# Attention: short score tiles on alternating bank pairs, new hand-written engine orders, and y copied and cleared by GpSimd

## The reference

```python
xn = layernorm(x) * gamma + beta
q, k, v = split(xn @ Wq, xn @ Wkv)            # 16 heads of 64
q, k = rope(q), rope(k)
sim = (q * 64 ** -0.5) @ k.T                  # causal mask
out = (softmax(sim) @ v) @ Wo
```

## Time and profile before

| | |
|---|---|
| device time, median of 3 runs | 2793.81 us (2791.97 to 2796.38) |
| the profiled execution's own time | 2805.46 us |
| its span, first to last instruction | 2803.7 us |
| attention, first A0 to last W3 on TensorE | 945 to 2316 us of the span |
| TensorE busy over the span | 90% |
| mean granted TensorE clock | 0.947 |

### The profile page before, as it was taken

The page is one execution under the profiler, slowest core; times in us unless marked ns, Lnnn a source line. Parts: engine busy times, 40 slices in busy tenths (PEclk is TensorE's granted clock), DMA queues, the critical chain, the costliest instruction groups (busy, mean ns, idle before and its releaser), DMA issues. The chain is left out here.

```text
span 2803.7 us, 45798 instructions
## 1 busy us (share of the span) xinstructions
PE 2537.3 (90%) x14626; PEld 1727.8 (62%) x14627; DVE 1312.9 (47%) x3173; ACT 1146.4 (41%) x2597; POOL 536.0 (19%) x479
## 2 busy tenths in 40 slices
PE   6999997999955699999999999999999995999992
PEld 6454544555535466665666656666666665999992
DVE  5445351122215455555556555655555652333335
ACT  3212111111113366665666656666566661222221
POOL 3000003444423233421111101101101100111113
PEclk7999998999975799999999999999999997999996
DMA  5010104865424422322111121111111106666795
GB/s 192 15 45 30 45 15 158 263 187 162 118 53 135 134 79 82 100 79 68 37 37 37 52 52 37 37 37 52 51 40 37 32 16 249 237 237 240 240 342 198
DMA packets 146334, 298.79 MB, mean 107 GB/s; under 512 B 16720, under 2 KB 104800, under 8 KB 135648
## 3 DMA queue, kind: packets, MB, share of 16 engines
q1 hardware_dynamic: 125280, 254.96, 28.6%
q0 software_dynamic: 20992, 43.07, 5.9%
HBM read 196.13 MB, written 68.30 MB: 94 GB/s over the span
## 5 line engine op out<-in xcount | busy, mean ns | idle before, releaser
L1347 DVE CUSTOM_DVE_ANT_0 at_p<-at_ps,atk_mask 128x640 f32<-128x640 f32 (+7 forms) x512 | 372.5, 750 | 304.3 <-PE at_ps L1201 168.8
L1258 ACT ACTIVATE at_p<-at_p,at_nmax 128x640 f32<-128x640 f32 (+7 forms) x512 | 394.2, 772 | 227.6 <-DVE at_nmax L1347 165.3
L1265 ACT ACTIVATE at_pT<-at_ps 128x512 f32<-128x512 f32 (+1 forms) x640 | 333.8, 550 | 186.1 <-PE at_ps L1211 183.0
L1290 POOL TENSOR_TENSOR at_qkT<-at_raw,at_swapped 128x1024 f32<-128x1024 f32 x64 | 151.3, 2364 | 1086.4 <-DVE at_swapped L1362 1086.1
L1201 PE MATMUL at_ps<-at_qkT 64*128 64x512 f32 (+3 forms) x1536 | 320.3, 522 | 19.3 <-DVE at_nmax L1347 15.3
L1211 PE MATMUL at_ps<-atk_ident,at_p 128*128 128x128 f32 x2304 | 323.6, 277 | 2.6 <-ACT at_raw L1271 1.9
L1211 PEld LDWEIGHTS at_ps<-atk_ident,at_p 128*128 128x128 f32 x2304 | 258.6, 141 | 109.0 <-issue 79.1
L1222 PE MATMUL at_ps<-at_pT,at_v 128*64 128x256 f32 (+1 forms) x2560 | 279.1, 365 | 0.1
L1498 PEld LDWEIGHTS moe_ps<-moe_xT,moe_w 128*128 128x128 f32 x2304 | 270.8, 193 | 5.2 <-ACT moe_xT L1531 1.6
L1498 PE MATMUL moe_ps<-moe_xT,moe_w 128*128 128x128 f32 x2304 | 271.4, 276 | 0.9 <-ACT moe_xT L1531 0.9
L1183 PE MATMUL at_ps<-atk_h,atk_w 128*128 128x512 f32 x512 | 250.3, 622 | 15.5 <-SPq L1074 15.2
(11 more groups left out here) (203 smaller groups left out, 3254.6 us busy)
## 6 DMA issues: line engine op xcount, KB each, us to landing
moe_w<-in_w_w SPq DMA_DIRECT2D x72, 1028.0 KB, 4.4
at_swapped<-at_raw SPq DMA_DIRECT2D x256, 128.0 KB, 2.3
atk_w<-in_w_qkv SPq DMA_DIRECT2D x32, 384.0 KB
slot_in<-ex_zero SPq DMA_DIRECT2D x9, 1032.0 KB
moe_xs<-slot_in SPq DMA_DIRECT2D x72, 129.0 KB
xn_n<-n_stage SPq DMA_DIRECT2D x8, 1024.0 KB, 4.6
ex_wg<-in_w_eg SPq DMA_DIRECT2D x16, 512.0 KB
ex_wu<-in_w_eu SPq DMA_DIRECT2D x16, 512.0 KB
```

The lines of the kernel that those rows point to most:

```text
L1258: act.activation(buf, buf, ACT.Exp, bias=nmax[:, unit:unit + 1], scale=-1.0, accum_out=rsum[:, unit:unit + 1]).then_inc(exp_done, 1)
L1265: act.activation(dst, ring[RING_BANK[part][ev]][:, 0:(i1 - i0) * P].rearrange("p (k c) -> p k c", c=P), ACT.Copy).then_inc(t_read, 1)
L1290: pool.tensor_tensor(out=qkT[x][:, :].rearrange("p (m t) -> p m t", m=2)[:, :, half * CH:(half + 1) * CH], in0=raw[half][:, :].rearrange(" ...
L1347: dve.tensor_tensor_reduce(out=p[unit % LAG][:, 0:(n[0] + 1) * P], in0=scores(*n), in1=mask[:, T - (n[0] + 1) * P:T], scale=-1.0, scalar=3 ...
```

## The change

Three things are changed.

Score tiles 0 to 3 alternate between the two banks of their head: even ones lie in banks 0 and 2, odd ones in banks 1 and 3. Tiles 4 to 7 need both. The wait of S2 and S3 is for the M two tiles back instead of one; S0 and S1 wait for the last M of the pair before. All three orders are new: TensorE's old one changes the array's form 22 times per iteration, the new one 17 times. The third thing is that `end(b)` moves from VectorE to GpSimd. It runs there after both rotations for the first pair of the next sequence, and VectorE's W0.0 waits for the clearing in every iteration, by a sequence number that `act_on` now gets.

```diff
--- before.py
+++ after.py
@@ -956,12 +956,12 @@
 QW = 2 * P
 HD = DH // 2
 
-PE_ORDER = ("T0.0 S2 A0+ T1.0 S3 V0 A1+ T2.0 A2+ T2.1 S4 T3.0 W0 T3.1 S5 A3+ T4.0 T4.1 T4.2 V1 S6 W1 A4+ A5+ T5.0 T5.1 S7 T5.2 T6.0 T6.1 A6+ T6.2 V2 "
-            "T6.3 T7.0 T7.1 T7.2 A7+ T7.3 S0+ W2 V3 S1+ W3")
-ACT_ORDER = ("E2.0 T0.0 T1.0 A0+ E2.1 E3.0 E3.1 A1+ T2.0 V0 T2.1 T3.0 E4.0 E4.1 T3.1 T4.0 E5.0 T4.1 V1 E5.1 T4.2 E6.0 A4+ A5+ E6.1 T5.0 T5.1 T5.2 "
-             "T6.0 T6.1 E7.0 E7.1 T6.2 T6.3 T7.0 T7.1 T7.2 V2 T7.3 E0.0+ V3 E0.1+ E1.0+ E1.1+")
-DVE_ORDER = ("M2.0 I0 M2.1 M3.0 M3.1 A2+ M4.0 M4.1 W0.0 W0.1 A3+ M5.0 M5.1 P0+ I1 I2 M6.0 W1.0 M6.1 W1.1 M7.0 M7.1 A6+ P1+ A7+ P2+ P3+ I3 M0.0+ W2.0 "
-             "M0.1+ W2.1 M1.0+ M1.1+ W3.0 W3.1")
+PE_ORDER = ("S2 S3 T0.0 A0+ T1.0 A1+ T2.0 A2+ T2.1 S4 V0 A3+ W0 S5 T3.0 T3.1 A4+ T4.0 T4.1 V1 S6 T4.2 A5+ W1 S7 T5.0 T5.1 T5.2 T6.0 A6+ T6.1 T6.2 "
+            "T6.3 V2 T7.0 T7.1 T7.2 T7.3 S0+ S1+ W2 V3 A7+ W3")
+ACT_ORDER = ("T0.0 E2.0 E2.1 T1.0 A0+ A1+ T2.0 T2.1 V0 E3.0 E3.1 E4.0 E4.1 T3.0 T3.1 T4.0 A4+ T4.1 E5.0 E5.1 V1 T4.2 E6.0 A5+ E6.1 T5.0 T5.1 T5.2 "
+             "T6.0 E7.0 T6.1 E7.1 T6.2 T6.3 V2 T7.0 T7.1 T7.2 T7.3 V3 E0.0+ E0.1+ E1.0+ E1.1+")
+DVE_ORDER = ("M2.0 M2.1 M3.0 M3.1 M4.0 A2+ M4.1 A3+ I0 W0.0 W0.1 M5.0 I1 P0+ M5.1 P1+ I2 M6.0 M6.1 W1.0 W1.1 M7.0 A6+ M7.1 W2.0 M0.0+ M0.1+ P2+ M1.0+ "
+             "W2.1 M1.1+ I3 P3+ A7+ W3.0 W3.1")
 
 
 def events(order):
@@ -1020,7 +1020,8 @@
 
         def scores(t, e):
 
-            return s.all_banks[:, e * 2 * CH:e * 2 * CH + (t + 1) * P]
+            at = e * 2 * CH + (t % 2 * CH if t < TB // 2 else 0)
+            return s.all_banks[:, at:at + (t + 1) * P]
 
         if scatter:
             rows = [s.sb(f"rows{u}", TB * ROW) for u in range(2)]
@@ -1042,23 +1043,21 @@
 
             return turned_before(n[0]) + n[1]
 
-        def run(eng, act_on, first_done=lambda: None, end=lambda b: None):
-
-            act_on("first", -1, -1, 1)
+        def run(eng, act_on, first_done=lambda: None):
+
+            act_on("first", -1, -1, 1, -1)
             first_done()
             if nb > 1:
                 with eng.Fori(0, nb - 1) as b:
                     with eng.Fori(0, PAIRS // 2) as i:
                         for u in range(2):
-                            act_on("both", b * PAIRS + (i * 2 + u), i * 2 + u, u)
-                    end(b)
+                            act_on("both", b * PAIRS + (i * 2 + u), i * 2 + u, u, b)
             it = (nb - 1) * PAIRS
             with eng.Fori(0, PAIRS // 2 - 1) as i:
                 for u in range(2):
-                    act_on("both", i * 2 + (it + u), i * 2 + u, u)
-            act_on("both", it + PAIRS - 2, PAIRS - 2, 0)
-            act_on("last", it + PAIRS - 1, PAIRS - 1, 1)
-            end(nb - 1)
+                    act_on("both", i * 2 + (it + u), i * 2 + u, u, nb - 1)
+            act_on("both", it + PAIRS - 2, PAIRS - 2, 0, nb - 1)
+            act_on("last", it + PAIRS - 1, PAIRS - 1, 1, nb - 1)
 
         s.start()
         with nc.Block() as block:
@@ -1192,13 +1191,13 @@
                         elif kind == "S":
                             if n % 4 == 0:
                                 pe.wait_ge(rot_done, of * 2 + n // 4 + 1 + ONE)
-                            if part != "first" or n > 0:
-                                pe.wait_ge(max_done, of * UNITS + 2 * n + ONE)
+                            if part != "first" or n > 1:
+                                pe.wait_ge(max_done, of * UNITS + 2 * (n if n >= TB // 2 else max(n - 1, 0)) + ONE)
                             width = (n + 1) * P
                             for at in range(0, width, CH):
                                 to = min(at + CH, width)
                                 for e in range(2):
-                                    last = pe.matmul(ps[2 * e + at // CH][:, 0:to - at], qkT[x][e * DH:(e + 1) * DH, n * P:(n + 1) * P],
+                                    last = pe.matmul(scores(n, e)[:, at:to], qkT[x][e * DH:(e + 1) * DH, n * P:(n + 1) * P],
                                                      qkT[x][e * DH:(e + 1) * DH, T + at:T + to], start=True, stop=True)
                                     if to == width:
                                         last.then_inc(s_ps, 1)
@@ -1297,6 +1296,13 @@
                         pool.indirect_dma_start(out=d.xd, out_offset=bass.IndirectOffsetOnAxis(ap=d.tok_slot[:, at:at + 1], axis=0),
                                                 in_=rows[of % 2][:, n * ROW:(n + 1) * ROW], in_offset=None).then_inc(sent, 16)
 
+                def end(b):
+                    pool.wait_ge(w_added, (b + 1) * (16 * PAIRS) + 16 + ONE)
+                    pool.wait_ge(y_out, b * 16 + ONE)
+                    pool.tensor_copy(y_stage[:, :], y[:, :]).then_inc(y_staged, 1)
+                    pool.wait_ge(y_staged, b + 1 + ONE)
+                    pool.memset(y[:, :], 0.0).then_inc(y_zero, 1)
+
                 assert scatter
                 load_rows(0)
                 pool.wait_ge(numbered, 16 + ONE)
@@ -1317,6 +1323,9 @@
                     rotate(of, 1)
                     if of < TOP * B:
                         send(of, range(TB // 2 if of > 0 else 0, TB))
+                    if of > 0 and of % PAIRS == 0:
+                        end(of // PAIRS - 1)
+                end(nb - 1)
                 pool.wait_ge(sent, 16 * TOP * NT)
 
             @block.vector
@@ -1325,16 +1334,7 @@
                 dve.sem_inc(w_added, 16)
                 dve.sem_inc(inv_done, 4)
 
-                def end(b):
-
-                    dve.wait_ge(w_added, (b + 1) * (16 * PAIRS) + 16 + ONE)
-                    dve.wait_ge(y_out, b * 16 + ONE)
-                    dve.tensor_copy(y_stage[:, :], y[:, :]).then_inc(y_staged, 1)
-                    dve.wait_ge(y_staged, b + 1 + ONE)
-                    dve.memset(y[:, :], 0.0).then_inc(y_zero, 1)
-                    dve.wait_ge(y_zero, b + 2 + ONE)
-
-                def act_on(part, it, pr, u):
+                def act_on(part, it, pr, u, seq):
                     for ev in part_of(DVE_ORDER, part):
                         kind, n, ahead = ev
                         of, x = it + ahead, (u + ahead) % 2
@@ -1364,6 +1364,8 @@
                         elif kind == "W":
                             n, e = n
                             bank = ring[RING_BANK[part][ev]]
+                            if n == 0 and e == 0:
+                                dve.wait_ge(y_zero, seq + 1 + ONE)
                             if e == 0:
                                 dve.wait_ge(inv_done, of * 4 + n + 5 + ONE)
                                 dve.wait_ge(w_ps, of * 4 + n + 1 + ONE)
@@ -1375,8 +1377,7 @@
                                 dve.scalar_tensor_tensor(out=part_y, in0=bank[:, t * C:(t + 1) * C], scalar=inv[:, unit:unit + 1], in1=part_y,
                                                          op0=ALU.mult, op1=ALU.add).then_inc(w_added, 1)
 
-                dve.wait_ge(y_zero, 1 + ONE)
-                run(dve, act_on, end=end)
+                run(dve, act_on)
 
 
 def moe(nc, d):
```

## The result

| | before | after |
|---|---|---|
| device time, median of 4 runs each | 2793.36 us | 2744.1 us |
| lowest to highest | 2791.97 to 2796.38 | 2737.67 to 2745.85 |
| the profiled execution's own time | 2805.46 us | 2745.85 us |
| attention, first A0 to last W3's end | 1371.1 us | 1312.3 us |

The ratio is 0.9818, with a 95% interval from 0.98 to 0.9836. The medians differ by 49.3 us; the ratio, which is taken from all the runs, stands for 50.8. The forecast was 2742, with 2729 to 2760 as its range.

A forecast was written before the change was run, and what follows sets the result against it. TensorE's own stream plus three stops at sequence starts bound attention. 34.1 + 17.7 + 2 - 2.5 = 51.3 us off 2805.46 gave 2754.2 for the profiled execution, 2742 for the median; range 2729 to 2760.

The forecast's parts named there:

- Fewer changes of form: TensorE's order per iteration: 17 form changes instead of 22, plus A7 covering V3's copy, saves 1.1 us, 34.1 in all.
- Rival (a): TensorE's form changes: only leaving a form is saved, 0.6 us per iteration, 18.6 us in all, giving 2758; 15%.
- (d): Rival: iterations save 1.4 us as waits for late copies inside the ring go too, first pairs gain all: 2730; 12%.
- The banks by themselves: Alternating score banks alone were costed at nothing; they let S2 and S3 stand together ahead of T0.0.
- The ends: At three sequence starts, moving y's copy and clearing to GpSimd removes TensorE's stops and gains the whole 17.7 us.
- GpSimd's durations: y on GpSimd: copy taken as 3.5 us, clearing as 2.4, with 2.5 us lost at the very end.
- The first eight pairs: Iterations with sends on GpSimd take 42.25 instead of 41.61; A7's cover may gain 0 to 4.5 us, 2 taken.
- Start and last iteration: New orders at the start and in the last iteration: counted as nothing for both, 3 us either way.
- The three close places: S7 after M6.1, S6 after M5.1, T7.3 after ScalarE's copy: first two hold, the third may cost 0.1 us per iteration.
- (c): Rival: the chain T4.2, M6, S7, or P0 ahead of M5.1, waits every iteration; at 2 us each it gives 2804; 3%.
- (e): Rival: new waits eat the saving from form changes while the sequence ends are gained: 2779; 5%.
- (b): Rival: GpSimd takes over 9.5 us for y or starts late, W0.0 holds TensorE, 12 us of stops stay: 2754; 8%.

The follow-up runs named there:

- the first experiment: The kernel before, run once more with no edit, for its profile: 2797.82 us, ratio 1.0004, its profiled execution 2797.29 us.

## Why the prediction was right, and where its terms were off

The sum is best checked against the quiet execution of before, the one of the first experiment: 2797.29 - 2745.85 = 51.4 us, where 51.3 were forecast. Neither of these two has the lateness in iterations 0 to 6; whether both ran on one chip isn't on record. The terms, from the iterations' lengths: 31 x 1.20 = 37.2 for the orders, 17.8 for the ends, 0.6 more in iteration 0; against it 1.2 at the start, 2.3 in the last iteration, 0.7 at the last copy. Together 51.4.

- **Fewer changes of form: right, a little too small.** 1.20 instead of 1.1 per iteration, 40.40 instead of 40.5. The price of a change (leaving 0.08, entering 0.06 to 0.11) was read from differences of starts; the runs that added two and two changes had 0.20 and 0.16 each, and the 1.20 less the 0.20 at V3's copy leave 0.20 for each of the five that went. Rival (a) is out: by it the iteration would be 41.0. So is (d), which had 40.2. Out too is the figure that was worked out from the Trainium skill ("TensorE: Matmul & The Clock Gate", "Step-by-step: what each phase is for"), an estimated 0.05 us per change: no run here comes near it. Why a change costs what it does isn't shown. That A7 covers V3's copy was right; without it W3 waits for 0.58.
- **The banks by themselves: nothing, right.** 0.9998, and iterations within a sequence stay at 41.6. That the new orders need these banks, as the prediction says, was not tested: no run has them in the old ones.
- **The ends: right, 17.7 whole.** GpSimd began straight behind its rotation, 3.1 us after W3's start where 3.0 were reckoned, and W0.0's adds came at 12.8, where W0 was to end at 12.5. The cover was there, 5.9 us of it unused, as four and eight clearings show from both sides. The parts add: by their ratios, orders and banks without this part gain 1.33% and this part alone 0.66%, 1.99% together; both at once gained 1.82% and, measured again, 1.90%, each with about 0.2% either way. By the traces attention gets 36.5 and 18.6 us shorter for the parts and 52.2 for both. Of the 2.9 that are missing 1.5 is a fall of the clock in the last iteration of that one execution, 0.5 is what the new orders take off the stops by themselves and so is counted twice, and 0.7 is a quicker start and iteration 0 in the profile with only y moved.
- **GpSimd's durations: too long.** 1.89 for the copy and 1.81 for the clearing, for my 3.5 and 2.4. I had taken the copy near a rotation with its two inputs. The loss at the end of attention is 0.7, not 2.5. The 1.8 us for the copy that was estimated from the Trainium skill ("GPSIMD Engine Reference", "Elementwise — side-by-side cycle accounting") was the nearer, and the measurement agrees with it.
- **The first eight pairs: the term had no cause.** The 42.25 isn't a cost of the kernel before that the new one removes: each of the two kernels has the lateness in one profile and lacks it in another, and in the experiments it goes by chip. The same lateness makes most of the offset: of the 8.2 us between before's two profiled executions, 6.6 lie in attention. The sum was made against this late execution and then lowered by the whole offset, so the lateness was taken off already, and the term's 2 us came off twice but for the 0.6 that iteration 0 did gain.
- **Start and last iteration: not zero.** From the first A0 to the first S2, where T0.0 stood first before, are 21.39 us instead of 20.17 (20.04 in the late execution). The chain to S0 did get shorter, 15.9 instead of 16.4, but S2 then stops 1.8 for a copy of VectorE. The last iteration takes 34.12 before and 36.38 or 34.90 after. Without the next pair's work between them dependent events stand closer, and the new order stops 1.8 for an exponential:

```profile
2223.80 0.85 PE L1210 MATMUL at_ps<-atk_ident,at_p 128*128 128x128 f32 x6 [1.80 <-ACT at_p L1257]
```

0.8 is the order's, 1.5 more a fall of the clock, which this profile has and the second lacks. The loss of both, 3.5 us, is a little more than the 3 either way that I had given them, and without the clock's fall 2.0.
- **The three close places.** In iteration 14 M6.1 is done at 1555.25 and S7 starts at 1555.57, straight behind W1: 0.3 us, with the hand-over of about 0.15 still in it, so less than the 0.4 that I had beyond the hand-overs. S6 has no wait either. T7.3 loses nothing that shows: the sixteen transposes of T7 take 1.93, those from T5.0 to T6.0 1.84, and the 0.09 between them is the leaving of the form. Rivals (c) and (e) are out, and so is (b), since the clearing ends 5.9 us ahead.

The orders were 3.1 and the last copy 1.8 better than their terms, the first pairs, the start and the last iteration 1.4, 1.2 and 2.3 worse. These cancel, and the closeness of 2742 to 2744 owes something to that luck.

## What to carry to other kernels

A form change of the array is worth counting when TensorE is the bound, but what stands between a producer and its consumer counts more: moving one event brought waits of 0.4 and 0.6 us per iteration where 0.16 to 0.40 of form changes were in play. A stop is removed by taking away the late work (here the copy and the clearing), not by letting the waiting instruction pass: in both runs that tried the latter it stopped again at the next thing that the late engine owed. Before a term is put on a small surplus, take a second profile, if possible on another chip: this one lay 11.65 us above the median of the timed runs, most of it through delays that the same kernel elsewhere didn't have.

## What had not been expected of the hardware

GpSimd copies 128 x 2048 float32 in 1.89 us where VectorE takes 1.23, and clears it in 1.81 where VectorE takes 1.76, so for a clearing the choice of engine costs nothing. A change of form costs 0.16 to 0.20 us at granted clock 1.00, in two runs that added them. In iterations in which GpSimd sends rows by indirect DMA, ScalarE's copies start up to 0.65 us late in all seven profiles from two chips and in none of the four from a third, 4 to 6 us over iterations 1 to 6; the cause stays open. And a stop of TensorE costs more than its length: 8.5 us for the 6.6 us in the run with eight clearings, with a granted clock of 0.93 over that iteration.
